# The last feed-forward in pairs of tiles, issued between the steps of the multi-head attention

## The chip, the cores and the metric

One core of one Trainium2 chip runs the whole program. The metric is device microseconds (us) of one execution; lower is better. Engines are called as in the profile: PE is TensorE (PEld its weight loads), DVE VectorE, ACT ScalarE, POOL GpSimd, SP the engine that issues the loads and stores here.

## The reference

Eight tiles of 128 tokens with 256 features go through two layers. Cut to what is computed:

```python
x = x + tanh(g_xattn[0]) * L0_xattn(layernorm(x), ctx, mask)       # stage A, one head
x = x + tanh(g_ffn[0])   * L0_ffn(layernorm(x), w1, w2, w3)        # stage B, quantised
x = x + tanh(g_xattn[1]) * L1_xattn(layernorm(x), ctx, ...)        # stage C, 16 heads, own layernorm of the result
x = x + tanh(g_ffn[1])   * L1_ffn(layernorm(x), w_gate, w_up, w_down)   # stage D
# L1_ffn: down(silu(x @ w_gate.T) * (x @ w_up.T)); hidden width 1024
```

All of it is fp32. Stage D splits each operand into a high and a low part in a one-pass matmul type and adds three products (high by high, low by high, high by low).

## The kernel before, in words

Each engine has one written order of instructions; semaphores join them. An engine that waits holds up everything behind it in its own order. The stages A, B and C go tile by tile: `step_c(t, p)` is called for t = 0 to 9 on every engine, and in one call each engine does its part for several tiles at different points of their way.

What happens to tile u in stage C, with the names used below:

- `xt_c(u)`: PE transposes the normed tile, ACT copies it out (`copy_ht`). `q(u)`: the query projection; ACT adds the bias and masks heads (`q_out`).
- `scores(u)`: PE writes banks 0 to 3; ACT takes four exponentials of 512 columns (`exp_c`); DVE clips the probabilities (L742, "the clip").
- `heads`: PE sums the probabilities of each head (head sums, bank 7) and multiplies them by the values (head values, bank 6). DVE takes the reciprocal of the sums (L728) and multiplies (OT, L735).
- PE multiplies by the output weights (`delta`, L1222, bank 5), DVE scales it (DL, L749), takes its mean and variance, POOL takes the power -0.5 (L373), DVE makes D2 (L762) and adds it to X (L769).
- Then the norm for stage D: statistics of X on DVE, power on POOL (L289), `norm_d` on DVE (XD, L714), two transposes on PE (XD), `hi_d` on ACT (L959), `lo_d` on DVE (L720). HTH and HTL, the two parts of the transposed tile, are what stage D reads.

Stage D goes over two groups of four tiles (TG = 512 tokens) and eight blocks of 128 hidden columns in each, 16 blocks n in all. `gate_up_d(n)`: 12 matmuls of 512 columns, gate into one bank and up into another, two pairs of banks in turn. ACT takes silu of gate (`silu_d`, L993), DVE multiplies by up (`gu_d`, L699), ACT rounds the high part (`hi_gu`, L997), DVE subtracts for the low part (`lo_gu`, L707), PE adds the block's share to the result (`down_d`, L1278, 12 matmuls of 256 columns). PE issues `down_d(n)`, then `gate_up_d(n + 2)`. At the end of each group DVE adds the result to X (`update_d`, L784), and SP stores pairs of tiles. Only two `gate_up_d` are issued inside the last steps of stage C:

```python
if t == NT:
    pe.wait_ge(c_ex, 4 * NT)
    gate_up_d(0)
...
for n in range(NG * FC):
    if n == 2:
        step_c(NT + 1, 1)
    down_d(n)
    if n + 2 < NG * FC:
        gate_up_d(n + 2)
```

ACT holds one table of functions: exp and silu lie in different ones, and `warm(func)` is a one-element call that brings the other table in ahead of use. Stage C runs under exp, stage D under silu, with one switch between them.

## Time and profile before

| | |
|---|---|
| median of 3 runs | 264.27 us (264.17 to 264.46) |
| the profiled execution | 264.11 us |
| its span (first to last instruction) | 262.3 us |
| granted PE clock, mean | 0.946 of full speed |
| PE busy | 212.0 us, 81% of the span |
| DVE, ACT, POOL busy | 181.0, 132.8, 83.9 us |

Stage C starts at about 127 us, the first block of stage D at 184.6 us, and the last matmul at 258.45 us. All times below are of the span of this one execution. A matmul's duration in the trace contains its way through the array, so the pace of a row of matmuls is read from one start to the next, not from the sum of durations.

### The profile page before, as it was taken

The page shows a single profiled execution, that of the slowest core. Times are in us where ns is not written, and L with a number is a line of the kernel's source. Part 1 is how long each engine was busy: PE and PEld are TensorE (multiplying, and loading weights), DVE is VectorE, ACT ScalarE, POOL GpSimd, SP SyncE. Part 2 cuts the span into 40 slices and gives each one's busy share as a digit, 9 for nine tenths or more (in the row PEclk, how much of TensorE's full clock was granted, in tenths as well). Part 3 has the DMA queues.
Part 4 walks back from the last instruction along what each step waited for, and adds up shares of the span by engine and source line. Part 5 has one row for each costly group of instructions (what it writes and reads, how often), then busy time and mean ns, then how long its engine had stood idle before and what let it go on. Part 6 is the DMA issues. An engine that isn't in the chain of part 4 may idle for free.

```text
span 262.3 us, 4538 instructions
## 1 busy us (share of the span) xinstructions
PE 212.0 (81%) x1658; PEld 174.5 (67%) x1658; DVE 181.0 (69%) x457; ACT 132.8 (51%) x296; POOL 83.9 (32%) x108
## 2 busy tenths in 40 slices
PE   0285557979889889897798688775999999999992
PEld 0264325858778778786576466654877888888882
DVE  2769879598988988786428999998984333262333
ACT  1138874478667667679755455553322323222220
POOL 2301111175856856868505333442100000000000
PEclk9999955699999999999959999997999999999999
DMA  5999003900000000000000000000000000020002
GB/s 169 369 390 301 5 0 139 343 1 0 2 0 0 2 1 0 2 2 0 0 2 2 0 2 4 0 4 0 2 2 0 0 0 2 0 80 2 0 0 80
DMA packets 9238, 12.55 MB, mean 48 GB/s; under 512 B 1025, under 2 KB 7937, under 8 KB 9217
## 3 DMA queue, kind: packets, MB, share of 16 engines
q1 hardware_dynamic: 8784, 12.07, 13.3%
q10 hardware_dynamic: 432, 0.20, 0.4%
q8 instruction: 13, 0.21, 0.3%
q14 instruction: 9, 0.07, 0.1%
HBM read 11.22 MB, written 1.05 MB: 47 GB/s over the span
## 4 chain that ended last, share of the span: by engine, by line
PE 50%; DVE 27%; ACT 7%; DMA 6%; issue 4%; POOL 3%; SPq 1%; DVEq 0%; ACTq 0%; POOLq 0%
PE PB L1259 16%; PE PB L1278 7%; DMA WRAW<-w_dram 6%; PE PB L1073 6%; PE PB L1172 4%; PE PB L1085 3%; DVE XV L524 3%; PE PB L1108 2%; PE PB L1112 2%; DVE HBQ L742 2%; PE PB L1019 2%; DVE RD L728 2%; DVE HBQ L572 2%; ACT SIL L906 2%; DVE HSD L578 2%
## 5 line engine op out<-in xcount | busy, mean ns | idle before, releaser
L1259 PE MATMUL PB<-SGN,WHI 128*128 128x512 f32 x128 | 40.5, 397 | 0.0
L1073 PE MATMUL PB<-SGN,XQH 128*128 128x512 f32 x64 | 27.7, 433 | 1.3 <-DVE XQL L553 1.3
L699 DVE TENSOR_TENSOR WRAW<-WRAW,PB 128x512 f32<-128x512 f32 x16 | 11.0, 686 | 24.0 <-ACT WRAW L993 23.9
L1278 PE MATMUL PB<-WHI,SGN 128*128 128x256 f32 x128 | 25.6, 283 | 2.2 <-DVE SGN L707 1.8
L1073 PE MATMUL PB<-SGN,XQL 128*128 128x512 f32 x64 | 27.1, 424 | 0.0
L289 POOL TENSOR_TENSOR RSTD<-MVS,MHALF 128x1 f32<-128x1 f32 x24 | 13.4, 560 | 40.9 <-DVE MVS L401 40.9
L1259 PEld LDWEIGHTS PB<-SGN,WHI 128*128 128x128 f32 x128 | 22.9, 188 | 4.5 <-issue 0.2
L1259 PE MATMUL PB<-SGN,WLO 128*128 128x512 f32 x64 | 25.2, 394 | 0.0
L993 ACT ACTIVATE WRAW<-PB 128x512 f32<-128x512 f32 x16 | 9.6, 600 | 28.0 <-PE PB L1259 28.0
L1278 PEld LDWEIGHTS PB<-WHI,SGN 128*128 128x128 f32 x128 | 20.7, 188 | 3.6 <-DVE SGN L707 2.4
L316 POOL TENSOR_TENSOR HBQ<-HBQ,HR 128x512 f32<-128x512 f32 x16 | 17.6, 1098 | 17.2 <-DVE HR L590 17.2
L906 ACT ACTIVATE SIL<-PB,WSC 128x512 f32<-128x512 f32 x16 | 11.0, 688 | 20.5 <-PE PB L1073 16.9
L322 POOL TENSOR_TENSOR HBQ<-HBQ,HSD 128x512 f32<-128x512 f32 x16 | 17.0, 1063 | 13.6 <-ACT HBQ L915 13.6
L572 DVE SCALAR_TENSOR_TENSOR HBQ<-PB,WSC,SIL 128x512 f32<-128x512 f32 x16 | 12.0, 747 | 10.9 <-ACT SIL L906 10.8
L707 DVE TENSOR_TENSOR SGN<-WRAW,SGN 128x512 fp32r<-128x512 f32 x16 | 11.1, 693 | 11.0 <-ACT SGN L997 11.0
L997 ACT CAST SGN<-WRAW 128x512 fp32r<-128x512 f32 x16 | 9.9, 620 | 17.1 <-DVE WRAW L699 17.1
L1019 PE MATMUL PB<-ident,XH 128*128 128x128 f32 x32 | 7.4, 327 | 13.6 <-DVE XH L417 13.6
L728 DVE RECIPROCAL RD<-PB 128x256 f32<-128x256 f32 x8 | 14.0, 1752 | 5.8 <-PE PB L1172 5.8
L1085 PE MATMUL PB<-SGN,HQH 128*128 128x256 f32 x64 | 18.0, 313 | 0.0
L1278 PE MATMUL PB<-WLO,SGN 128*128 128x256 f32 x64 | 17.9, 280 | 0.0
L1172 PE MATMUL PB<-HBQ,ONE 128*32 128x128 f32 x256 | 10.2, 308 | 9.0 <-DVE D L762 9.0
L966 ACT ACTIVATE HBQ<-PB 128x512 f32<-128x512 f32 x32 | 17.5, 616 | 0.0
(122 smaller groups left out, 545.7 us busy)
## 6 DMA issues: line engine op xcount, KB each, us to landing
WRAW<-w_dram SPq DMA_DIRECT2D x2, 2048.0 KB, 12.1
X<-x_dram SPq DMA_DIRECT2D x2, 512.0 KB, 5.8
CTXT<-ctxt_dram SPq DMA_DIRECT2D x1, 1024.0 KB, 9.6
CTX<-ctx_dram SPq DMA_DIRECT2D x1, 1024.0 KB, 12.0
WRAW<-w_dram SPq DMA_DIRECT2D x1, 1024.0 KB, 14.9
WQK<-wqkvo_dram SPq DMA_DIRECT2D x1, 1024.0 KB, 7.8
WRAW<-wd_dram SPq DMA_DIRECT2D x1, 1024.0 KB, 10.1
out_dram<-X SPq DMA_DIRECT2D x4, 256.0 KB, 2.2
```

The lines of the kernel that those rows point to most:

```text
L289: nc.gpsimd.tensor_tensor(RSTD[:, bass.ds(t, 1)], MVS[:, bass.ds(t, 1), 1], MHALF[:], ALU.pow).then_inc(rstd_ready, 1)
L316: nc.gpsimd.tensor_tensor(h, h, spread(HR, p, half), ALU.mult).then_inc(b_v, 1)
L322: nc.gpsimd.tensor_tensor(halves(HQ, p, half), halves(HB, p, half), spread(HSD, p, half), ALU.mult).then_inc(b_hq, 1)
L572: nc.vector.scalar_tensor_tensor(out=h_part(p, half), in0=PB[2 * half + 1][:], scalar=WSC[:, 1:2], in1=SIL[:, half, :], op0=ALU.mult, op1= ...
L728: nc.vector.reciprocal(RD[:], PB[7][:, 0:D]).then_inc(c_rd, 1)
L906: nc.scalar.activation(SIL[:, half, :], PB[2 * half][:], ACT.Silu, scale=WSC[:, 0:1]).then_inc(b_sil, 1)
L966: nc.scalar.activation(PR[:, p, b * 512:(b + 1) * 512], PB[b][:], ACT.Exp, scale=1.0 / math.sqrt(HD)).then_inc(c_ex, 1)
L1073: mm = nc.tensor.matmul(PB[2 * half + m][:], part[:, p, c, :], sgn(m, c, a, b), start=(c == 0 and k == 0), stop=(c == DC - 1 and k == 1))
L1085: mm = nc.tensor.matmul(PB[7][:, 0:D], part[:, j, :], sgn3(j), start=(j == 0 and i == 0), stop=(j == FC - 1 and i == 1))
L1172: mm = nc.tensor.matmul(PB[bank][HB32 * j:HB32 * (j + 1), c * P:(c + 1) * P], parts(h), PR[:, p, head_at(h):head_at(h) + P], start=(e == 0 ...
L1259: mm = nc.tensor.matmul(PB[2 * b + m][:], wcol(w_part, m, c, j), act_part[:, c, g * TG:(g + 1) * TG], start=(c == 0 and i == 0), stop=(c = ...
L1278: mm = nc.tensor.matmul(down_bank(g, k), act_part[:, b, ts], wdown(w_part, j), start=(j == 0 and i == 0 and k % 2 == 0), stop=(j == FC - 1 ...
```

## The change

Stage D works on pairs of tiles (TG = 256 tokens, four groups of eight blocks, 32 blocks n). Gate and up of a block share one bank, 256 columns each. Blocks up to n = 16 use bank 6 alone; later ones take turns between banks 6 and 0. `down_d` has 6 matmuls of 256 columns. Four buffers instead of two hold the products.

The blocks are issued inside `step_c`: in step t, n = 4t - 14, each engine does its part of blocks n to n + 3 among its work for stage C, and of `down_d` blocks n - 3 to n; t runs to 11. The first blocks, 0 and 1, fall into step 3; blocks 2 to 13 into steps 4 to 6; the attention's own work ends with step 9.

To make room in PSUM, head sums and head values share bank 5 with `delta`, the transposes of XD move to bank 4 (shared with `xt_c` and `q`), and the result of `down_d` has bank 7. The reciprocal waits for the head values (c_pv) instead of for the sums alone.

The exponentials of tile t + 1 are taken in step t instead of step t + 1. The mean and variance of DL, D2, the update of X, and the statistics of X of a tile move one step later on DVE, to the start of the step, and `norm_d` and `lo_d` follow in the same step. ACT switches tables twice in each of the steps 3 to 6 (exp for the four exponentials, silu after them), and once more in step 3.

PE's order in a step t from 4 to 6 is: `down_d(n-3)`, `q(t+1)`, `down_d(n-2)`, `gate_up_d(n)`, head sums (t-1), XD transposes (t-2), `gate_up_d(n+1)`, head values (t-1), `down_d(n-1)`, `gate_up_d(n+2)`, `scores(t+1)`, `xt_c(t+2)`, `gate_up_d(n+3)`, `delta(t-1)`, `down_d(n)`.

The core of the diff (DVE's order first, then ACT's, then two functions of PE, whose order is given above; of the removed lines only the first stand here):

```diff
-TG = 512
-NG = NT * P // TG
-TPG = TG // P
+TPG = 2
+TG = TPG * P
+NG = NT // TPG
+NB = 4
+SPT = NG * FC // NT
+LEAD = 14
+LAST = (LEAD + NG * FC) // SPT + 1
...
+        def gu_bank(n):
+            return PB[6] if n <= SPT * NT // 2 or n % 2 == 0 else PB[0]
+        def ffn(n):
+            return 0 <= n < NG * FC
...
-                sp.wait_ge(x_done, 2 * i + 3 * NT + 2)
+                sp.wait_ge(d_x, i + 1)
...
+            def update_d(g):
+                dve.wait_ge(d_dn, FC * (g + 1))
+                xs = X[:, TPG * g:TPG * (g + 1), :].rearrange("p t d -> p (t d)")
+                nc.vector.scalar_tensor_tensor(
+                    out=xs, in0=PB[7][:], scalar=TANHG[:, 3:4], in1=xs, op0=ALU.mult,
+                    op1=ALU.add).then_inc(d_x, 1)
...
             def step_c(t, p):
+                n = SPT * t - LEAD
+                if live(t - 2):
+                    dve.wait_ge(c_de, t - 1)
+                    nc.vector.bn_stats(ST2[:], DL[:]).then_inc(c_st, 1)
+                    dve.wait_ge(c_st, t - 1)
+                    nc.vector.bn_aggr(MV2[:], ST2[:]).then_inc(c_mv, 1)
+                    dve.wait_ge(c_mv, t - 1)
+                    nc.vector.tensor_scalar(VE2[:], MV2[:, 1:2], LN_EPS, None, ALU.add
+                                            ).then_inc(c_ve, 1)
+                if n > FC and (n - 2) % FC == 0:
+                    update_d((n - 2) // FC - 1)
+                if live(t - 2):
+                    nc.vector.scalar_tensor_tensor(
+                        out=D2[:], in0=DL[:], scalar=MV2[:, 0:1], in1=GAM[:],
+                        op0=ALU.subtract, op1=ALU.mult).then_inc(c_d2, 1)
+                if ffn(n - 1):
+                    gu_d(n - 1)
+                if live(t - 2):
+                    dve.wait_ge(c_d2, t - 1)
+                    dve.wait_ge(c_r2, t - 1)
+                    dve.wait_ge(c_xb, t - 1)
+                    nc.vector.scalar_tensor_tensor(
+                        out=X[:, t - 2, :], in0=D2[:], scalar=RSTD2[:], in1=X[:, t - 2, :],
+                        op0=ALU.mult, op1=ALU.add).then_inc(x_done, 1)
+                    stats(t - 2, p, t - 2 + 2 * NT)
+                if ffn(n - 1):
+                    lo_gu(n - 1)
+                if ffn(n):
+                    gu_d(n)
+                if live(t - 2):
+                    norm_d(t - 2)
+                if ffn(n):
+                    lo_gu(n)
+                if live(t - 2):
+                    lo_d(t - 2)
                 if live(t + 2):
                     norm(t + 2, p, 2)
+                if ffn(n + 1):
+                    gu_d(n + 1)
+                if live(t - 1):
...
+                if ffn(n + 1):
+                    lo_gu(n + 1)
+                if ffn(n + 2):
+                    gu_d(n + 2)
                 if live(t):
...
+                if ffn(n + 2):
+                    lo_gu(n + 2)
                 if live(t - 1):
                     dve.wait_ge(c_dl, t)
...
+            def silu_d(n):
+                act.wait_ge(d_gu, n + 1)
+                nc.scalar.activation(SG[:, n % NB, :], gu_bank(n)[:, 0:TG], ACT.Silu
+                                     ).then_inc(d_sil, 1)
+            def hi_gu(n):
+                act.wait_ge(d_g, n + 1)
+                need(act, d_dn, n - NB + 1)
+                nc.scalar.copy(GUH[:, n % NB, :], GU[:, n % NB, :]).then_inc(d_gh, 1)
...
             def step_c(t, p):
+                n = SPT * t - LEAD
+                switch = ffn(n + 3) and live(t + 1)
                 if live(t + 1):
                     q_out(t + 1)
+                if ffn(n):
+                    silu_d(n)
+                    hi_gu(n)
+                if live(t - 2):
+                    hi_d(t - 2)
+                if ffn(n + 1):
+                    silu_d(n + 1)
+                    hi_gu(n + 1)
+                if switch and not ffn(n + 2 - SPT):
+                    warm(ACT.Silu)
+                if ffn(n + 2):
+                    silu_d(n + 2)
+                if switch:
+                    warm(ACT.Exp)
+                if live(t + 1):
+                    exp_c(t + 1, 1 - p, 0)
+                if ffn(n + 2):
+                    hi_gu(n + 2)
+                if live(t + 1):
+                    exp_c(t + 1, 1 - p, 1)
                 if live(t + 2):
                     copy_ht(t + 2, p, 4, xt_done, c_q, c_ht, 2 * NT)
+                if live(t + 1):
+                    exp_c(t + 1, 1 - p, 2)
+                    exp_c(t + 1, 1 - p, 3)
+                if switch:
+                    warm(ACT.Silu)
+                if ffn(n + 3):
+                    silu_d(n + 3)
+                    hi_gu(n + 3)
             warm(ACT.Exp)
             copy_ht(1, 1, 4, xt_done, c_q, c_ht, 2 * NT)
...
+            for b in range(4):
+                exp_c(0, 0, b)
+            for t in range(LAST):
+                step_c(t, t % 2)
...
+            def xd_t(u):
+                pe.wait_ge(d_ln, u + 1)
+                need(pe, d_hl, u)
+                pe.wait_ge(c_qm, 4 * min(u + 4, NT))
+                transpose_x(XD[:], 4, d_t)
+            def gate_up_d(n):
+                g, j = n // FC, n % FC
+                if j == 0:
+                    pe.wait_ge(d_hl, TPG * (g + 1))
+                if n == SPT * NT // 2 + 1:
+                    pe.wait_ge(c_ex, 4 * NT)
+                elif n > SPT * NT // 2:
+                    pe.wait_ge(d_g, n - 1)
+                else:
+                    need(pe, d_g, n)
+                for m in range(2):
+                    terms = ((HTH, WHI), (HTL, WHI), (HTH, WLO))
...
```

## Rows read from the trace of the kernel before

**Rows 1.** The chain that ended last: shares of the span by engine

```profile
PE 50%; DVE 27%; ACT 7%; DMA 6%; issue 4%; POOL 3%; SPq 1%; DVEq 0%; ACTq 0%; POOLq 0%
```

**Rows 2.** Busy time in stretches of stages C and D

```profile
core 0: us, PE busy (x) PEld busy (x) DVE busy (x) ACT busy (x) POOL busy (x), PEclk, DMA share, GB/s
...
131.70:139.50 7.80, 7.34 (x91) 5.77 (x90) 2.96 (x5) 3.84 (x9) 1.02 (x2) 0.56 0.01 2
...
153.90:161.10 7.20, 5.60 (x96) 4.54 (x96) 6.96 (x16) 4.10 (x10) 2.77 (x6) 1.00 0.00 1
...
212.00:231.00 19.00, 19.00 (x113) 16.66 (x112) 6.21 (x9) 6.09 (x10) 0.00 (x0) 1.00 0.00 1
```

**Rows 3.** Timeline of one steady step of stage C (start, duration, instruction)

```profile
151.90 1.75 DVE L728 RECIPROCAL RD<-PB 128x256 f32<-128x256 f32 x1
...
156.89 1.52 ACT L898 ACTIVATE QM<-PB,BQM,PAR 128x128 f32<-128x128 f32 x4
...
157.83 0.49 DVE L769 SCALAR_TENSOR_TENSOR X<-D,RSTD,X 128x256 f32<-128x256 f32 x1
...
157.94 1.08 PE L1172 MATMUL PB<-HBQ,ONE 128*32 128x128 f32 x32 [1.43 <-DVE D L762]
...
159.10 1.75 DVE L728 RECIPROCAL RD<-PB 128x256 f32<-128x256 f32 x1
159.26 0.55 POOL L289 TENSOR_TENSOR RSTD<-MVS,MHALF 128x1 f32<-128x1 f32 x1 [1.56 <-DVE MVS L401]
```

**Rows 4.** Timeline of the start of stage C

```profile
125.97 1.09 ACT L966 ACTIVATE HBQ<-PB 128x512 f32<-128x512 f32 x2
...
126.93 1.05 PE L1160 MATMUL PB<-HT,WQK 128*128 128x128 f32 x8
...
129.47 1.10 ACT L966 ACTIVATE HBQ<-PB 128x512 f32<-128x512 f32 x2
...
132.72 2.08 PE L1160 MATMUL PB<-HT,WQK 128*128 128x128 f32 x8 [0.46 <-ACT HT L821]
...
136.73 1.76 DVE L728 RECIPROCAL RD<-PB 128x256 f32<-128x256 f32 x1 [4.84 <-PE PB L1172]
...
140.87 0.48 DVE L749 SCALAR_TENSOR_TENSOR DL<-PB,RES,BO 128x256 f32<-128x256 f32 x1 [0.62 <-PE PB L1222]
```

**Rows 5.** Timeline of one steady block of stage D

```profile
217.60 0.64 PE L1259 MATMUL PB<-SGN,WHI 128*128 128x512 f32 x2
...
220.41 0.28 PE L1278 MATMUL PB<-WHI,SGN 128*128 128x256 f32 x1
...
220.60 0.60 ACT L993 ACTIVATE WRAW<-PB 128x512 f32<-128x512 f32 x1 [2.24 <-PE PB L1259]
...
221.81 0.64 PE L1259 MATMUL PB<-SGN,WHI 128*128 128x512 f32 x2
```

**Rows 6.** Timeline around the two switches of ACT's table

```profile
124.09 1.28 ACT L813 ACT_TABLE_LOAD   x1
...
125.62 0.37 ACT L821 COPY HT<-PB 128x256 f32<-128x256 f32 x1
...
185.33 1.28 ACT L813 ACT_TABLE_LOAD   x1
...
187.80 0.60 ACT L993 ACTIVATE WRAW<-PB 128x512 f32<-128x512 f32 x1 [0.97 <-PE PB L1259]
```

**Rows 7.** Groups of instructions by line and shape (count, busy, mean ns of one)

```profile
L735 DVE TENSOR_TENSOR OT<-PB,RD 128x256 f32<-128x256 f32 x8 | 3.4, 419 | 0.1
...
L959 ACT CAST SGN<-PB 128x256 fp32r<-128x256 f32 x8 | 3.0, 372 | 16.6 <-PE PB L1019 16.6
```

**Rows 8.** Timeline of the end

```profile
258.07 1.66 DVE L784 SCALAR_TENSOR_TENSOR X<-PB,TANHG,X 128x256 f32<-128x256 f32 x4 [1.06 <-PE PB L1278]
...
258.45 0.28 PE L1278 MATMUL PB<-WHI,SGN 128*128 128x256 f32 x1
```

More of the change, by code:

```diff
@@ L999, in _ @@
[L999 to L1009 removed]
+            for b in range(4):
+                exp_c(0, 0, b)
+            for t in range(LAST):
+                step_c(t, t % 2)
         @block.tensor
@@ L1192, in scores, with head_sums, head_values, delta @@
                             mm.then_inc(c_s, 1)
+            def head_sums(u, p):
+                pe.wait_ge(c_p, u + 1)
+                need(pe, c_de, u)
+                heads(0, lambda h: ONE2[:, h % 2, :], p)
+            def head_values(u, p):
+                pe.wait_ge(c_v, 2 * u + 2)
+                heads(D, lambda h: V1[:, p, h, :], p).then_inc(c_pv, 1)
+            def delta(u):
+                pe.wait_ge(c_o, u + 1)
+                for c in range(DC):
+                    mm = nc.tensor.matmul(PB[5][:, 0:D], OT[:, c * P:(c + 1) * P],
+                                          WQK[:, 3, c, :], start=(c == 0), stop=(c == DC - 1))
+                mm.then_inc(c_dl, 1)
@@ new lines, in xd_t @@
+            def xd_t(u):
[15 more added lines that the diff above has]
+                    terms = ((HTH, WHI), (HTL, WHI), (HTH, WLO))
+                    for c in range(DC):
+                        for i, (act_part, w_part) in enumerate(terms):
+                            mm = nc.tensor.matmul(
+                                gu_bank(n)[:, m * TG:(m + 1) * TG], wcol(w_part, m, c, j),
+                                act_part[:, c, g * TG:(g + 1) * TG],
+                                start=(c == 0 and i == 0), stop=(c == DC - 1 and i == 2))
+                mm.then_inc(d_gu, 1)
@@ new lines, in down_d @@
+            def down_d(n):
+                g, j = n // FC, n % FC
+                pe.wait_ge(d_gl, n + 1)
+                if j == 0:
+                    need(pe, d_x, g)
+                for k in range(TPG):
+                    ts = slice(k * P, (k + 1) * P)
+                    terms = ((GUH, WHI), (GUH, WLO), (GUL, WHI))
+                    for i, (act_part, w_part) in enumerate(terms):
+                        mm = nc.tensor.matmul(
+                            PB[7][:, k * D:(k + 1) * D], act_part[:, n % NB, ts],
+                            wdown(w_part, j), start=(j == 0 and i == 0 and k == 0),
+                            stop=(j == FC - 1 and i == 2), skip_group_check=True)
+                mm.then_inc(d_dn, 1)
@@ L1215, in step_c @@
                     xt_c(t + 2, p)
-                if t == NT:
-                    gate_up_d(1)
+                if t >= NT:
+                    down_d(n)
+                if ffn(n + 3):
+                    gate_up_d(n + 3)
                 if live(t - 1):
-                    pe.wait_ge(c_o, t)
-                    need(pe, c_de, t - 1)
-                    for c in range(DC):
-                        mm = nc.tensor.matmul(PB[5][:, 0:D], OT[:, c * P:(c + 1) * P],
-                                              WQK[:, 3, c, :], start=(c == 0),
-                                              stop=(c == DC - 1))
-                    mm.then_inc(c_dl, 1)
-                if live(t - 2):
-                    pe.wait_ge(d_ln, t - 1)
-                    if not live(t - 1):
-                        pe.wait_ge(d_hl, t - 2)
-                    transpose_x(XD[:], 7, d_t)
+                    delta(t - 1)
+                if t < NT and ffn(n):
+                    down_d(n)
+                if t >= NT:
+                    down_d(n + 1)
             pe.wait_ge(b_xl, NT)
```

194 lines of the change are left out of this document (45 added, 149 removed).

## Prediction

> **What bounds the kernel now.** I read the chain that ended last first: half of it is PE and a quarter DVE [rows 1], so no single engine explains the span and the stages have to be taken apart. The windows do that [rows 2]. In a steady step of stage C DVE is busy 6.96 of 7.20 us and PE 5.60. In stage D, once it runs, PE is busy all the time. So stage C waits for DVE, stage D for PE, and running them side by side could in principle fill PE's 1.6 us of idle time per step of C.
>
> The steady timeline gives the pace: one reciprocal to the next is 7.20 us [rows 3]. A block of stage D takes 221.81 - 217.60 = 4.21 us for 12 matmuls of 512 columns (220.41 - 217.60 = 2.81, so 234 ns each) and 12 of 256 columns (1.40, 117 ns each) [rows 5]. A column costs the same in both widths.
>
> PE's side of the ledger: from q(1) at 126.93 [rows 4] to the end of the last matmul, 258.45 + 0.28 [rows 8], are 131.8 us. The work in it is 16 x 4.21 = 67.4 for stage D and 8 x 5.60 less some 2.8 for what was issued earlier (q(0), scores(0), two transposes) = 42.0. That is 109.4 us. The other 22.4 us are waits and a half clock. The change has to bring that number down. It cannot touch the 109.4.
>
> **Part by part: PE's work.** The change doubles the number of gate and up matmuls at half the width: 32 x 12 x 0.117 = 44.9 us, as 16 x 2.81 before, and `down_d` stays at 32 x 6 x 0.117 = 22.5. Cost nothing, on the row. The doubled weight loads (192 more) lie under the matmuls, as they do in the 256-column `down_d`, whose pace is exactly half; without that cover 192 x 0.188 (a weight load's own time there) would be 36 us, which the 117 ns excludes.
>
> **ACT and DVE per block.** For 256 columns I take 0.40 us for an ACT operation (0.372 for the 256-column cast) and 0.42 for a DVE one (0.419) [rows 7]. Both engines together do more small instructions than before, but neither is full: DVE 7.2 + 8 x 0.42 = 10.6 us a step, ACT 4.1 + 8 x 0.40 and two switches. What counts is the order in which they answer PE.
>
> **The table switches.** A load takes 1.28 us, and 125.62 - 124.09 = 1.53 us pass from its start to the next operation [rows 6]. I take 1.53. The other switch has 2.47 us to the next operation, but there 0.97 of it is a wait for PE, so 2.47 is the upper bound. Nine switches replace one. ACT's idle time covers their sum (about 14 us); their place does not hide them all, as the next part shows. The Trainium skill ("ScalarE: Activation LUTs", What ACT_TABLE_LOAD costs, and its rule to batch by table set) speaks against the edit: it gives 1283 ns for the load, which the trace shows, and some 1380 ns of draining besides, 2.66 us for each switch. No row shows that drain. By the page's price each switch would take 1.13 us more, two in each of four steps, and the sum would come to about 273.
>
> **An interleaved step (t = 4 to 6), walked in order.** PE has 13.95 us of work: four gate_up of 1.40, four `down_d` of 0.70, 5.55 for attention (5.60 in the row [rows 2]; split by starts in the steady step: q 1.0, head sums 0.87 of the 1.08 shown [rows 3], values 1.0, scores 1.05, `xt_c` 0.35, delta 0.95, XD 0.35). Set 0 at the start of `gate_up_d(n+3)` of the step before. PE goes on with delta, down, down, q, down until 5.45 and then needs bank 6 free, that is `gu_d` of that last block. Its silu stands on ACT behind a chain that starts with the silu of the block before (gate_up from -2.8; its result 1.6 later, since silu followed 0.19 after the last matmul was issued, 220.60 against 220.41 [rows 5]; silu to -0.8): switch to exp (0.76), exponential, `hi_gu`, exponential, `copy_ht`, two exponentials at 0.545 each [rows 4] (3.65), switch to silu (5.18), silu (5.57), `gu_d` (6.02). With 0.1 for a start after a wait, PE goes on at 6.1: **0.65 us lost**. The second place: after gate_up(n) and head sums PE is free at 8.37 for the XD transposes, which need `norm_d`. On DVE that stands behind `gu_d(n)`, which needs silu(n), which on ACT stands behind `q_out` (1.4, from 6.45) [rows 3]: silu ends 8.24, `gu_d` 8.69, `norm_d` 9.06, transposes 9.15: **0.78 us lost**. After that PE runs through (values, down, gate_up, scores, transposes) to the next gate_up at 15.4. So a step costs 15.4 us. The same work before cost 7.20 + 4 x 2.11 = 15.6. The interleaving as such gives only 0.2 us a step; a PE without waits would give 1.65.
>
> **The start (steps 0 and 1).** All four exponentials of tile 0 now run at once, 125.97 to 128.15, where the second pair waited to 129.47 [rows 4]. q(2) then starts at about 131.4 and not 132.72. In that stretch the granted clock was 0.56, the lower level of 1.2 GHz for most of it, after a thinly used PE, and it came back after PE had been full [rows 2]. I let it fall again: q(2) 2.0, head sums 1.6, values 1.0 at the restored clock, ending at 136.0. The reciprocal now needs the values, so it starts at 136.1 and not at 136.73, and DL of tile 0 at 139.5 and not 140.87. A gain of 1.4; half a microsecond if the values are slow too.
>
> **Steps 2 and 3, without cover.** Here the moved chain stands bare on DVE. The update of X waits for POOL's power (0.25). `norm_d` comes right after the statistics, and from the update's start to the end of the second power are 159.81 - 157.83 = 1.98 us, where DVE has 1.27 of work [rows 3]: 0.7 lost. `lo_d` comes right after `norm_d` and waits for PE's transposes and ACT's cast: 1.5 from start to start where 0.4 is work: 1.1 lost. Before, the clip and the reciprocal (1.75) lay over these waits. With 0.15 for delta that makes 9.4 us from DL of tile 0 to that of tile 1, at 148.9, against 7.2 a step before. In step 3 the first gate_up waits for the same `lo_d` and starts at 6.05 after DL, scores follow, and the second gate_up starts at 8.85: 157.75.
>
> **The sum.** Second gate_up of step 3 at 157.75; of step 4, 5 and 6 at 173.2, 188.6 and 203.65 (step 6 has one transpose pair less). From there 49.75 us of PE work remain (19 gate_up, 22 `down_d`, three tiles' rest). To it come 1.35 (no q to cover the switch to silu in step 7) and 0.6, 1.4 and 1.95 at the XD transposes of tiles 5, 6 and 7, where `norm_d` again ends DVE's chain of some 4 us after DL; and 0.5 before the last `down_d`. That ends PE at 259.1, and 22.5 us of waits stand where 22.4 stood. The last update is one instruction of 512 columns, at most the 0.83 that two tiles took [rows 8]: 259.95, against 258.07 + 1.66 = 259.73. So the profiled execution goes from 264.11 to 264.3; the median stood 0.16 above it: **264.5 us**.
>
> **Rivals.** (a) *The waits find cover and PE binds.* If `norm_d` and the silu are ready a little earlier than my walk has them, the interleaved steps fall towards 13.95: three times 1.43 gone is 4.3 us, **260.2**. For it: each wait is under 0.8 us, two or three instructions long. Against: both hang on ACT's written order. It decides where a step takes under 15.2.
> (b) *The clock falls in steps 2 and 3*, and this is the case on the other side. PE works in bursts there, with two gaps of over 1.5 us, as it did in bursts ahead of the fall at the start [rows 2, 4]; in the steady step, with a longest gap of 1.43 [rows 3], the clock stayed at 1.00 [rows 2]. At half rate the two gate_up, scores and delta in the path (1.4 + 1.4 + 1.1 + 1.0) take up to 4.9 more; with part of the stretch covered I take 3: **267.5**. It decides from the point at which a gate_up of step 3 takes over 2 us.
> (c) *A switch costs the upper bound*, 2.47: 0.94 more, twice in the chain that PE waits for, four times: 7.5 us, **272**. The rule on draining in the Trainium skill's page on ScalarE's tables would do this. The 1.53 us at the switch without a wait speak against it.
>
> **Chances.** Forecast case, gains and waits cancelling to within 1.5 us: 0.45 (faster 0.14, same 0.16, slower 0.15). (a) 0.25, (b) 0.24, (c) 0.06. Faster by over 0.2% (half a microsecond, about what a measurement of this kernel can tell): 0.14 + 0.25 = 0.39. Same 0.16. Slower 0.15 + 0.24 + 0.06 = 0.45. The range takes in (a) and (b) with little to spare: 260.0 to 268.0, leaving out (c) and the ends of (a) and (b), about 0.18. My forecast's own range is 263.0 to 266.0.
>
> **What the profile after would show.** Right: the second gate_up of one step to that of the next 15.2 to 15.6 us; PE waiting for DVE's `gu_d` before the first gate_up of a step and for `norm_d` before XD's transposes, 0.6 to 0.8 each; eight or more loads of 1.28 us; the DVE step from DL 0 to DL 1 over 9 us; gate_up at 117 ns a matmul. Wrong: PE over 95% busy from step 4 on (then (a)); a clock under 0.9 between 140 and 160 us (then (b)); silu over 2 us after a load's start (then (c)); or 256-column gate_up slower than 117 ns, which would add 4.5 us for each 10% and is the one term I hold certain.

## The result, and the profile after

| | before | changed |
|---|---|---|
| median | 264.37 us (264.17 to 264.83, 4 runs) | 268.41 us (267.57 to 269.21, 4 runs) |
| profiled execution, its span | 264.11, 262.3 us | 267.57, 265.8 us |
| mean granted clock | 0.946 | 0.949 |

The ratio is 1.015, with an interval of 1.0113 to 1.0188: the changed kernel is 1.5% slower, and 0.4 us past the upper end of the range. Its four executions, from the fastest to the slowest, have mean clocks of 0.949, 0.949, 0.939 and 0.932; the profiled one is the fastest, so the 0.8 us from it to the median are not profiled. The forecast for the profiled execution was 264.3, so 3.3 us have to be found in it. Ratios, and the medians below, leave out executions more than 1.5% above the fastest of their kernel: three of the nine of e1, its profiled one among them, and two of before's.

The start of stage C, from the timeline (it answers to [rows 4]; the load to [rows 6]):

```profile
125.35 1.28 ACT L820 ACT_TABLE_LOAD   x1
...
127.23 2.06 ACT L973 ACTIVATE HBQ<-PB 128x512 f32<-128x512 f32 x4
...
128.20 1.06 PE L1179 MATMUL PB<-HT,WQK 128*128 128x128 f32 x8
...
133.04 1.16 PE L1179 MATMUL PB<-HT,WQK 128*128 128x128 f32 x8 [1.05 <-ACT HT L828]
...
136.16 1.76 DVE L783 RECIPROCAL RD<-PB 128x256 f32<-128x256 f32 x1 [4.40 <-PE PB L1191]
...
139.60 0.48 DVE L801 SCALAR_TENSOR_TENSOR DL<-PB,RES,BO 128x256 f32<-128x256 f32 x1
```

All four exponentials run at once, as drawn. Two things were not drawn. The load itself stands at 125.35 and not at 124.09, though nothing ahead of it was changed. And q(2) takes 1.16 us, not 2.08: here the clock did not fall. The two cancel, and DL of tile 0 comes at 139.60 (forecast 139.5).

Then the steps. PE's timeline from step 3 on, first the waits of steps 3 and 4, then the last gate_up, `gate_up_d(n + 3)`, of steps 3 to 6. It is the second one of step 3 and the fourth of the others; the prediction says "second" of all, but its walk goes from one `gate_up_d(n + 3)` to the next.

```profile
154.27 0.44 PE L1037 MATMUL PB<-ident,XD 128*128 128x128 f32 x2 [2.12 <-DVE XD L730]
155.63 0.50 PE L1251 MATMUL PB<-SGN,WHI 128*128 128x256 f32 x2 [0.92 <-DVE SGN L736]
...
164.44 0.50 PE L1251 MATMUL PB<-SGN,WHI 128*128 128x256 f32 x2 [1.51 <-DVE WRAW L708]
...
167.40 0.44 PE L1037 MATMUL PB<-ident,XD 128*128 128x128 f32 x2 [0.25 <-DVE XD L730]
```

```profile
158.53 0.48 PE L1251 MATMUL PB<-SGN,WHI 128*128 128x256 f32 x2
...
173.82 0.48 PE L1251 MATMUL PB<-SGN,WHI 128*128 128x256 f32 x2
...
189.06 0.48 PE L1251 MATMUL PB<-SGN,WHI 128*128 128x256 f32 x2
...
204.10 0.51 PE L1251 MATMUL PB<-SGN,WHI 128*128 128x256 f32 x2
```

Forecast were 157.75, 173.2, 188.6 and 203.65. Up to 204 us the profile is 0.45 us behind the walk. The rest of the 3.3 us lies behind that. PE's timeline there, and the windows around it (columns as in [rows 2]):

```profile
239.10 0.53 PE L1037 MATMUL PB<-ident,XD 128*128 128x128 f32 x2 [2.12 <-DVE XD L730]
239.29 0.77 PE L1251 MATMUL PB<-SGN,WHI 128*128 128x256 f32 x2
...
242.00 0.41 PE L1267 MATMUL PB<-WHI,SGN 128*128 128x256 f32 x1
...
243.04 0.40 PE L1251 MATMUL PB<-SGN,WHI 128*128 128x256 f32 x2
...
245.19 0.40 PE L1251 MATMUL PB<-SGN,WHI 128*128 128x256 f32 x2
...
246.62 0.28 PE L1267 MATMUL PB<-WHI,SGN 128*128 128x256 f32 x1
```

```profile
236.00:239.00 3.00, 0.98 (x9) 0.78 (x7) 2.54 (x9) 1.09 (x3) 1.00 (x2) 1.00 0.01 3
239.00:242.00 3.00, 2.90 (x15) 2.90 (x16) 0.80 (x3) 0.37 (x1) 0.00 (x0) 0.55 0.00 0
242.00:243.00 1.00, 1.00 (x7) 1.00 (x7) 0.35 (x1) 0.38 (x1) 0.00 (x0) 0.64 0.05 16
243.00:251.00 8.00, 8.00 (x69) 8.00 (x68) 3.60 (x9) 2.70 (x7) 0.00 (x0) 1.00 0.10 33
```

PE waits 2.12 us for `norm_d` of tile 7, and on the far side the granted clock is 0.55, close to the lower level of 1.2 GHz. The gate_up that starts at 239.29 takes 242.00 - 239.29 = 2.71 us and the `down_d` after it 1.04; in the block of 245.19, at full clock, these are 1.43 and 0.71. That is 1.6 us gone beside the wait itself. A block at full clock takes 2.14 us here, where half a block of before took 2.11 [rows 5].

The end, from the timeline (it answers to [rows 8]):

```profile
261.45 0.39 PE L1267 MATMUL PB<-WHI,SGN 128*128 128x256 f32 x1 [0.41 <-DVE SGN L715]
...
262.48 0.75 DVE L722 SCALAR_TENSOR_TENSOR X<-PB,TANHG,X 128x512 f32<-128x512 f32 x1 [1.08 <-PE PB L1267]
```

### The profile page after: what moved, and what is told of

Its sections match the earlier page's. It is cut to its first block and busy times, and to the rows that moved or that the text cites. A ratio compares the mean times of both kernels' runs of the same rounds, so it can differ in the third digit from the quotient of the medians.

```text
span 265.8 us, 5038 instructions
## 1 busy us (share of the span) xinstructions
PE 216.3 (81%) x1850; PEld 185.1 (70%) x1850; DVE 185.8 (70%) x485; ACT 150.2 (57%) x344; POOL 84.8 (32%) x108
## 5 line engine op out<-in xcount | busy, mean ns | idle before, releaser
L1251 PE MATMUL PB<-SGN,WHI 128*128 128x256 f32 x256 | 49.7, 291 | 3.8 <-DVE WRAW L708 2.9
L1251 PEld LDWEIGHTS PB<-SGN,WHI 128*128 128x128 f32 x256 | 40.2, 193 | 5.2 <-DVE WRAW L708 4.0
L1251 PE MATMUL PB<-SGN,WLO 128*128 128x256 f32 x128 | 36.6, 286 | 0.0
L1267 PE MATMUL PB<-WHI,SGN 128*128 128x256 f32 x128 | 29.0, 297 | 0.5 <-DVE SGN L715 0.4
L978 ACT ACTIVATE WRAW<-PB 128x256 f32<-128x256 f32 x32 | 12.3, 385 | 27.5 <-PE PB L1251 27.4
L708 DVE TENSOR_TENSOR WRAW<-WRAW,PB 128x256 f32<-128x256 f32 x32 | 13.4, 419 | 18.5 <-ACT WRAW L978 18.5
L984 ACT CAST SGN<-WRAW 128x256 fp32r<-128x256 f32 x32 | 12.9, 405 | 21.4 <-DVE WRAW L708 21.4
L1251 PEld LDWEIGHTS PB<-SGN,WLO 128*128 128x128 f32 x128 | 24.6, 192 | 0.0
L382 POOL TENSOR_TENSOR RSTD<-VE,MHALF 128x1 f32<-128x1 f32 x8 | 5.4, 678 | 53.1 <-DVE VE L749 53.1
L715 DVE TENSOR_TENSOR SGN<-WRAW,SGN 128x256 fp32r<-128x256 f32 x32 | 13.5, 422 | 8.5 <-ACT SGN L984 7.9
## 6 DMA issues: line engine op xcount, KB each, us to landing
WRAW<-w_dram SPq DMA_DIRECT2D x2, 2048.0 KB, 12.2
CTX<-ctx_dram SPq DMA_DIRECT2D x1, 1024.0 KB, 12.2
```

Source lines behind the costliest of these rows:

```text
L708: nc.vector.tensor_tensor(GU[:, b, :], SG[:, b, :], gu_bank(n)[:, TG:2 * TG], ALU.mult).then_inc(d_g, 1)
L715: nc.vector.tensor_tensor(GUL[:, b, :], GU[:, b, :], GUH[:, b, :].bitcast(F32), ALU.subtract).then_inc(d_gl, 1)
L978: nc.scalar.activation(SG[:, n % NB, :], gu_bank(n)[:, 0:TG], ACT.Silu).then_inc(d_sil, 1)
L984: nc.scalar.copy(GUH[:, n % NB, :], GU[:, n % NB, :]).then_inc(d_gh, 1)
L1251: mm = nc.tensor.matmul(gu_bank(n)[:, m * TG:(m + 1) * TG], wcol(w_part, m, c, j), act_part[:, c, g * TG:(g + 1) * TG], start=(c == 0 and ...
L1267: mm = nc.tensor.matmul(PB[7][:, k * D:(k + 1) * D], act_part[:, n % NB, ts], wdown(w_part, j), start=(j == 0 and i == 0 and k == 0), stop ...
```

## The experiments

Each kernel runs with before on the same chip; before had medians of 263.96 beside e1 to e4, 264.12 beside e5 to e8, 264.19 beside e9 and e10, and 264.18 beside e11. "Over before" is the difference of the two medians, and kernels are compared by it. The first columns are of these runs; the others are of the profiled execution, in us counted from its exp table load: DL of tiles 0, 1 and 7, and the end of the last update.

| kernel | median | over before | ratio to before | load at | DL 0 | DL 1 | DL 7 | end |
|---|---|---|---|---|---|---|---|---|
| before | 264.37 | | | 124.09 | 16.78 | 24.44 | 69.39 | 135.64 |
| before again (e0) | 264.59, one run | | | 124.52 | 16.78 | 24.45 | 69.47 | 135.72 |
| changed | 268.41 | 4.0 | 1.0113 to 1.0188 | 125.35 | 14.25 | 24.07 | 108.82 | 137.88 |
| e1 no switch | 265.08 | 1.1 | 1.0017 to 1.0087 | 125.50 | 15.83 | 26.60 | 108.39 | 137.41 |
| e2 XD later | 264.22 | 0.3 | 0.9973 to 1.0026 | 125.22 | 15.86 | 26.30 | 108.93 | 135.49 |
| e3 keep clock | 266.31 | 2.4 | 1.0064 to 1.0116 | 124.82 | 14.23 | 25.00 | 109.66 | 137.19 |
| e4 pairs only | 268.24 | 4.3 | 1.0144 to 1.0237 | 125.58 | 15.71 | 23.35 | 66.09 | 137.38 |
| e5 early exp | 262.24 | -1.9 | 0.9900 to 0.9958 | 124.53 | 15.11 | 22.77 | 67.01 | 133.27 |
| e7 step later | 272.22 | 8.1 | 1.0269 to 1.0373 | 124.59 | 14.24 | 25.00 | 105.13 | 141.62 |
| e8 fill early | 263.84 | -0.3 | 0.9956 to 1.0011 | 124.30 | 16.84 | 26.34 | 108.98 | 135.53 |
| e9 fill start | 261.47 | -2.7 | 0.9831 to 0.9922 | 124.84 | 13.51 | 21.16 | 66.26 | 132.49 |
| e10 tanh | 267.36 | 3.2 | 1.0074 to 1.0154 | 125.18 | 15.84 | 26.28 | 110.43 | 138.51 |
| e11 all mended | 262.76 | -1.4 | 0.9920 to 0.9976 | 126.06 | 14.23 | 23.74 | 106.37 | 132.95 |

**The 1.26 us ahead of the load.** Two kernels ask whose they are: before once more, and before with 192 narrow matmuls at its end, so that it has as many PE instructions as the changed one.

> The kernel before, unchanged, for one more profile of it. Theory 1 (the 1.3 us by which the changed kernel's profile is later at the first exp table load are the place of the clock's half stretch in stages A and B, which moves from run to run): the load lies somewhere between 124.1 and 125.6 us, and the half stretch between 20 and 55 us with it. Rival (they belong to the changed program): it stands at 124.1 us again, within 0.1.

> The kernel before with 192 more matmuls of 32 columns at its end, into a bank that nothing reads: as many TensorE instructions as the changed kernel has, and some 6 to 10 us more work at the end, so its time says nothing. What is read is the first exp table load, which stands at 124.09 us in before and at 124.82 to 125.58 us in the changed kernel and its four variants. Theory 1 (a longer program moves the first loads, and the clock's half stretch with them): it stands at 125.2 us or later. Rival (it is the clock's half stretch of that one run, or of those kernels for another reason): it stays at 124.1 us, or lies wherever the half stretch between 20 and 55 us of that run puts it.

The load stood at 124.52 in the first and at 125.03 in the second; in e5 and e9, the same as before up to there, at 124.53 and 124.84. Windows of before and then of before again:

```profile
20.00:30.00 10.00, 5.30 (x30) 3.67 (x28) 9.06 (x42) 8.74 (x33) 1.67 (x3) 1.00 0.64 189
30.00:40.00 10.00, 5.64 (x17) 2.87 (x17) 7.54 (x31) 7.60 (x26) 1.71 (x3) 0.64 0.00 0
```

```profile
20.00:30.00 10.00, 5.48 (x31) 3.85 (x29) 9.09 (x42) 8.74 (x33) 1.66 (x3) 0.99 0.64 189
30.00:40.00 10.00, 6.51 (x16) 3.72 (x17) 7.17 (x31) 7.64 (x26) 1.70 (x3) 0.50 0.00 0
```

The stretch at half clock in stages A and B does not start in the same place in each execution, and moves all that follows. From the load on, the two executions of before agree to 0.1 us. The load is at 124.09 to 125.03 in the five profiles that have before's program up to there and its groups of four, at 124.30 to 126.06 in the nine others. In all fourteen it is later the longer the stretch lasts: the mean clock from 20 to 60 us is 0.79 in before (load at 124.09), 0.74 in three (124.30 to 124.53), 0.70 in seven (124.59 to 125.35), 0.66 in two (125.50 and 125.58) and 0.62 in e11 (126.06). So e0's theory 1 held; of e6 the theory (125.2 or later) missed and the rival held, by which the load lies where the stretch puts it. The second group's mean is higher by 0.5 us (125.13, without e4, against 124.60); whether the changed program lengthens the stretch stays open. The 192 matmuls of e6 took 38.2 us where 6 to 10 were expected; the last section comes back to them. All comparisons of profiles below count from the load.

**The clock in the tail (e3).** Idle matmuls ahead of the XD transposes of steps 8 and 9:

```diff
+                if live(t - 2) and t >= NT:
+                    for _ in range((6, 16)[t - NT]):
+                        nc.tensor.matmul(PB[1][:, 0:TG], wcol(WHI, 0, 0, 0), HTH[:, 0, 0:TG],
+                                         start=True, stop=True)
                 if live(t - 2):
                     xd_t(t - 2)
```

> The changed kernel with 6 and 16 idle matmuls of 256 columns into a free bank ahead of the transposes of XD in steps 8 and 9, so that PE is busy while it waits. Theory (the wait itself is unchanged, but the clock falls after it and costs 1.5 us): gate_up 23 takes 1.43 instead of 2.71 us and the time falls by 1 to 2 us. Rival (the clock falls anyway or the fall is not what separates the runs): within 0.5 us of the changed kernel, or slower.

266.31, 2.4 us over before where the changed kernel is 4.0 over: 1.7 us less, as its theory had it. The same place in its windows, PE filled and the clock whole:

```profile
235.00:238.00 3.00, 3.00 (x28) 3.00 (x27) 2.66 (x9) 0.69 (x2) 0.72 (x1) 1.00 0.01 3
238.00:241.00 3.00, 2.79 (x25) 2.59 (x23) 1.93 (x6) 0.78 (x2) 0.68 (x1) 1.00 0.02 5
241.00:244.00 3.00, 3.00 (x28) 3.00 (x27) 0.97 (x3) 1.17 (x3) 0.00 (x0) 1.00 0.00 0
```

From DL of tile 7 to the end are 27.53 us and not 29.06: 1.53 us, the 1.6 read above. So the price of the fall is shown twice over. That the fill is what kept the clock does not follow from this one profile, because the clock can stay whole without it. e1 has the same wait of 2.12 us there and the same fall; e7 waits 2.23 us, unfilled, and has none:

```profile
235.06 0.44 PE L1037 MATMUL PB<-ident,XD 128*128 128x128 f32 x2 [2.23 <-DVE XD L730]
```

```profile
232.00:235.00 3.00, 0.82 (x6) 0.62 (x6) 2.71 (x10) 1.09 (x3) 0.68 (x1) 1.00 0.26 87
235.00:238.00 3.00, 2.94 (x25) 2.95 (x26) 1.18 (x4) 0.92 (x3) 0.00 (x0) 1.00 0.00 0
```

The count of filled and open waits in the last section speaks for the fill.

**The order around XD (e2).** PE takes gate_up(n+1) ahead of the transposes; ACT takes silu(n+1) ahead of `hi_d`, DVE the norm and `gu_d(n+1)` ahead of `lo_d`. PE's part:

```diff
-                if live(t - 2):
-                    xd_t(t - 2)
                 if ffn(n + 1):
                     gate_up_d(n + 1)
+                if live(t - 2):
+                    xd_t(t - 2)
```

> The changed kernel with the transposes of XD one place later on PE (after gate_up n+1), and hi_d and lo_d one place later on ACT and DVE. Theory (PE stands still for norm_d although work is ready): the waits of 0.25 three times, 0.24, 0.94 and 2.12 us before these transposes shrink to under 1 us in all, and with them goes the fall of the clock after the longest; the time falls by 2.5 to 4 us, to about 265. Rival (the work behind, gate_up n+1 and then gate_up 24, waits for gu_d and lo_d instead): less than 1 us is gained.

264.22: 3.8 us less over before than the changed kernel, level with before, as its theory had it. PE's waits from 160 to 260 us, in all, times, longest:

```profile
PE PB L1252 <- DVE WRAW L708: 2.9, 3, 1.5
PE PB L1038 <- DVE XD L730: 0.7, 1, 0.7
PE PB L1268 <- DVE SGN L715: 0.4, 1, 0.4
```

The XD waits are down to one of 0.7, the clock stays whole in the tail (26.56 us from DL 7 to the end), and this with a worse start, where the clock did fall (DL 0 at 15.86).

**The switches (e1, e10).** e1 takes exp of gate in place of silu and has no loads in the steps; it leaves silu out, and only its time counts.

> The changed kernel without its nine extra switches of ACT's table: the silu of the feed-forward is replaced by an exponential, so that all of it runs under one table (the output is therefore not that of the reference). Theory (switches in ACT's order hold up PE at the start of a step): PE's waits before the first gate_up of steps 4 and 7 (1.51 and 1.07 us in the changed kernel's trace) and the 0.31 of step 5 go, and the time falls by 2.5 to 3.5 us to about 265. Rival (the waits only move on to the transposes of XD, because norm_d is late anyway): less than 1 us is gained. A second rival, that each switch costs more than the 1.5 us seen: more than 5 us is gained.

265.08, 2.9 us less over before than the changed kernel, as its theory had it. PE's waits for the product and for XD from 160 us to the end, in the changed kernel and then in e1: the first go, the second stay, so the rival is out.

```profile
PE PB L1251 <- DVE WRAW L708: 2.9, 3, 1.5
PE PB L1037 <- DVE XD L730: 4.0, 6, 2.1
```

```profile
PE PB L1245 <- DVE WRAW L708: 0.6, 1, 0.6
PE PB L1031 <- DVE XD L730: 4.2, 6, 2.1
```

Its profiled execution has a mean clock of 0.923, with falls ahead of 154 us and again at 239; the steps between these, at full clock, from DL 2 to DL 5 (38.29, 52.38, 67.05, 81.83 us after the load), take 14.1, 14.7 and 14.8 us, against 15.3, 15.25 and 15.05 (35.76, 51.05, 66.30, 81.35). So the switches cost about 2 us over these three steps. e10 takes them away in a kernel that computes silu: the Trainium skill ("ScalarE: Activation LUTs", Table sets: the hidden batching unit) puts exp and tanh in one set, and this case's profile agrees (its first stage takes both under one load). DVE pays with one more instruction a block, on top of e2:

```diff
-                nc.vector.tensor_tensor(GU[:, b, :], SG[:, b, :], gu_bank(n)[:, TG:2 * TG],
-                                        ALU.mult).then_inc(d_g, 1)
+                nc.vector.scalar_tensor_tensor(
+                    out=SG[:, b, :], in0=SG[:, b, :], scalar=1.0, in1=gu_bank(n)[:, 0:TG],
+                    op0=ALU.add, op1=ALU.mult).then_inc(d_s1, 1)
+                dve.wait_ge(d_s1, n + 1)
+                nc.vector.scalar_tensor_tensor(
+                    out=GU[:, b, :], in0=SG[:, b, :], scalar=0.5, in1=gu_bank(n)[:, TG:2 * TG],
+                    op0=ALU.mult, op1=ALU.mult).then_inc(d_g, 1)
```

> The variant with the XD transposes behind the second gate and up block (264.2 us), with silu(g) worked out as g / 2 * (1 + tanh(g / 2)): exp and tanh lie in one table (the profile shows a tanh and the exponentials of the first stage with no load between), so the switches in steps 3 to 6 fall away, and VectorE takes one more instruction of 256 columns for each block. Theory 1 (the switches cost some 2 us, as the variant without them suggested, and VectorE has room): a step of the interleaved ones falls from 15.0 to about 14.4 us and the time to 262.0 to 263.2. Rival (VectorE's added 0.45 to 0.5 us a block stands in the same chain from gate and up to the freed bank, and takes the gain back): 264 to 265.5 us, with longer waits of TensorE for VectorE's product ahead of gate and up.

267.36, 3 us more than e2 and past its rival too. Its waits from 160 to 260 us:

```profile
PE PB L1252 <- DVE WRAW L713: 3.3, 7, 1.0
PE PB L1038 <- DVE XD L736: 1.6, 2, 1.4
PE PB L1252 <- DVE SGN L742: 0.5, 1, 0.5
```

The wait for the product comes seven times instead of three, 0.4 us more in all, and those at XD are 0.9 us longer. ACT's switches were cheaper than 0.42 us more on DVE in each block.

**The parts alone (e4, e5, e7).** e4 is before with pairs of tiles (TG = 256, gate and up still in two banks), nothing interleaved. e5 is before with the exponentials a step earlier. e7 is the changed kernel with LEAD = 18, four blocks fewer between the steps and four more behind them.

```diff
-                if live(t):
-                    exp_c(t, p, 0)
-                    exp_c(t, p, 1)
                 if live(t + 1):
                     q_out(t + 1)
-                if live(t):
-                    exp_c(t, p, 2)
-                    exp_c(t, p, 3)
+                    exp_c(t + 1, 1 - p, 0)
+                    exp_c(t + 1, 1 - p, 1)
                 if live(t + 2):
                     copy_ht(t + 2, p, 4, xt_done, c_q, c_ht, 2 * NT)
+                if live(t + 1):
+                    exp_c(t + 1, 1 - p, 2)
+                    exp_c(t + 1, 1 - p, 3)
```

> The kernel before with pairs of tiles alone (TG = 256, four groups, gate and up in banks of their own, the blocks behind the attention as before, nothing interleaved). Theory (a 256-column gate_up matmul takes 119.5 ns here and not 117): 384 times 2.5 ns is 1.0 us slower than before, about 265.3. Rival (the narrower matmul costs nothing, as my prediction had it): within 0.4 us of before. A second rival: four groups also need shorter waits at the end, and it is faster by 0.5 to 1.

> The kernel before with one part of the change alone: the exponentials of tile t+1 are issued in step t (those of tile 0 ahead of step 0). The feed-forward, its groups of four tiles and its two banks stay where they were. Theory 1 (the start pays as forecast): the first residual (DL of tile 0) comes 1.2 to 1.4 us earlier than the 140.87 us of the profiled run of before, counted from the first exp table load, and the kernel ends about 1.2 us sooner: 262.5 to 263.2 beside the 264.0 of before on this chip. Rival (TensorE sets the pace anyway, or the clock takes it back): the steady steps keep their 9.4 to 9.8 us and the end comes within 0.4 us of before. Whichever holds, the place of the exp table load tells about the shift ahead of the attention: this kernel has the same instructions as before up to there, so it should stand at 124.1 us if the shift of 1.3 us in the changed kernels belongs to them, and anywhere from 124 to 125.6 us if it moves from run to run.

> The changed kernel with the whole feed-forward one step later (18 in place of 14 blocks behind), so that four blocks fewer lie between the attention's steps. Theory 1 (a block between the steps costs as much TensorE time as one behind them, 2.14 us, and the steps only hide 0.2 to 0.4 us of waits each): 268 to 269 us, within 0.5 us of the changed kernel's 268.4. Rival (the interleaving does hide waits, about 2 us a step): 270 to 271 us.

e4 is slower by as much as the whole change, 4.3 us, and its theory and both rivals missed. Its blocks take 2.14 us instead of 2.11, and at the change of stages, where two blocks are in flight, a block of half the work covers half as much of the chain over ACT and DVE; PE's waits there:

```profile
192.30 0.36 PE L1276 MATMUL PB<-WHI,SGN 128*128 128x256 f32 x1 [0.68 <-DVE DL L749]
...
196.42 0.38 PE L1276 MATMUL PB<-WHI,SGN 128*128 128x256 f32 x1 [1.73 <-DVE SGN L707]
```

Before has 0.45 and 0.40 in these two places. The profiled execution is the fastest of its four and ends 1.75 us later than before's, counted from the load; the load is 1.49 us later besides. Where the rest of the 4.3 lies was not profiled. e5 is faster by 0.7%, 1.9 us, more than its theory's 1.2. DL 0 comes 1.7 us earlier after the load (1.2 to 1.4 expected); how much of that is the order and how much a shorter stretch at half clock there (the windows below) is not separated. Its profile gains another 0.7 between DL 5 and DL 6, where the clock fell in before (0.52 from 179.5 to 183 us) and not in e5. In e7 the rival held, by a little more than its figures: 4.0 us slower over before than the changed kernel. The four blocks are 8.56 us of PE work; taken from between the steps they shorten the time to DL 7 by 3.7 us and lengthen the tail by 7.4. So blocks between the steps do hide waits, about a microsecond each. The two profiles have falls of the clock in different places, e7 from 145 to 162 us and the changed one at 239; without them 3.7 would be some 4.6 (DL 0 to DL 1 takes 0.95 longer in e7) and 7.4 some 9.0, an estimate, with much the same difference.

**Filling the other falls (e8, e9, e11).** e8 is e2 with idle matmuls in the waits of steps 1 to 3. e9 is e5 with 8 of them ahead of scores(1) and 8 ahead of q(2). e11 is e8 with those two as well.

```diff
             def step_c(t, p):
+                if t == 1:
+                    for _ in range(8):
+                        nc.tensor.matmul(PB[5][:, 0:D], wcol(WHI, 0, 0, 0), WHI[:, 1, 0:D],
+                                         start=True, stop=True)
                 if live(t + 1):
                     q(t + 1, 1 - p)
+                if t == 0:
+                    pe.wait_ge(b_hl, 2 * NT)
...
```

> The variant in which the transposes of XD come behind the second gate and up block of a step, with idle 256-column matmuls put where TensorE waits in the first steps: 7 ahead of the output projection of steps 1 and 2, 16 and 8 ahead of the XD transposes of steps 2 and 3. Theory 1 (the half clock at 133 to 138 us and 147 to 154 us of that variant costs what TensorE does there at half speed, and comes from its waits): the clock stays whole from 126 us to the end, and the time falls by 1.5 to 2.5 us from 264.2 to 261.7 to 262.7 us, under both kernels. Rival (VectorE's chain of the first steps sets the time there, at either clock): within 0.5 us of 264.2 us. A third: the idle matmuls themselves come late and hold up the work behind them: 264.5 to 265.5 us.

> The kernel before with the exponentials one step earlier (262.24 us on this chip) and, besides, 8 idle 256-column matmuls ahead of scores(1) and 8 ahead of q(2), where TensorE waits about 1.0 us each. Theory 1 (the half clock at 131 to 137 us comes from these waits, and costs q(2) and the head sums there 1.7 us, which the first DL passes on): the granted clock stays whole from 126 to 145 us, the first DL comes 14.0 us after the exp table load and not 15.1, and the time falls by about 1 us, to 261.0 to 261.6. Rival (the clock falls there whatever TensorE does in these two gaps): within 0.3 us of 262.24, the first DL at 15 to 16 us after the load.

> The interleaved kernel with everything mended that the runs have shown so far: the XD transposes behind the second gate and up block, idle matmuls in the waits of steps 1 to 3 (263.8 us with these two), and the 8 and 8 idle matmuls ahead of scores(1) and q(2) that kept the clock whole at the start of the plain kernel with early exponentials (261.47 us there). Theory 1 (the early exponentials and the whole clock give the gain, the interleaving of pairs gives nothing beside them): the first DL comes 13.5 us after the exp table load where it came 14.3 to 16.8, the end some 132.5 to 133.5 us after the load, and the time is 261.0 to 262.3, level with 261.47. Rival (the interleaving earns its own 1 to 2 us once the clock is whole): 259.3 to 260.5 us. A third (VectorE's chain in steps 2 and 3 eats the earlier start): 263 to 264 us.

e8 gained nothing that can be told from no change. The clock stood whole from 138.2 us on, but had fallen before that (0.53 from 131 to 138.2), and the step from DL 0 to DL 1 is 9.5 us at full clock as well: there DVE's chain is the limit, its rival. e9 has the lowest median of this study, 261.47, and its theory held; its interval and that of e5 just overlap. Windows of e5, then of e9:

```profile
126.00:132.00 6.00, 4.16 (x42) 2.77 (x34) 2.79 (x6) 5.13 (x13) 3.42 (x5) 1.00 0.00 0
132.00:138.00 6.00, 5.71 (x88) 4.76 (x88) 1.94 (x3) 2.72 (x8) 1.02 (x3) 0.72 0.01 3
```

```profile
126.00:132.00 6.00, 5.95 (x64) 4.76 (x57) 3.04 (x8) 5.12 (x13) 3.33 (x6) 1.00 0.00 0
132.00:138.00 6.00, 5.73 (x98) 4.48 (x96) 3.23 (x4) 4.31 (x12) 1.87 (x4) 1.00 0.01 3
```

PE filled in the first row, the clock whole in the second, DL 0 1.6 us earlier. The end gains 0.8: between DL 5 and DL 6 half of it is given back (7.85 us in place of 7.00). There PE waits 2.3 us ahead of the head sums of tile 7 in both, and behind it the clock fell in e9 and not in e5. Windows of e5, then of e9:

```profile
177.00:180.00 3.00, 1.80 (x64) 1.72 (x64) 2.83 (x9) 0.00 (x0) 1.03 (x2) 1.00 0.00 0
```

```profile
177.00:180.00 3.00, 3.00 (x60) 3.00 (x64) 2.15 (x5) 0.00 (x0) 1.25 (x2) 0.50 0.02 5
```

e11 beats both kernels too, at 262.76, 0.5 us over the upper end of its theory 1 and under the third's; its DL 0 comes at 14.23 and not at 13.5. From the load its end is 132.95, beside 132.49 of e9, although its clock stood whole from 126 to 258 us and that of e9 did not. Beside the early exponentials and the idle matmuls the interleaving of pairs, as it stands here, has no gain to show.

## Why the prediction was wrong

- **Ahead of the change**: the sum took the load's place from one execution of before. It moved by 1.26 us in the changed kernel's, by 0.4 in a second one of before, and by 0.9 in one with the same program up to there (e6). No term stood for that, and it is over a third of the 3.3 us. A term of the other sign hides it up to DL 0: the clock that stayed at the start (below) gives 1.1 us back.
- **"Cost nothing, on the row"**, for gate_up in 256 columns, "the one term I hold certain": 1.435 us a block, 119.5 ns a matmul and not 117. Over 32 blocks 32 x 1.435 - 16 x 2.81 = 1.0 us, 5 ns for each of the 192 added matmuls. The forecast took the 117 ns of `down_d`'s 256 columns for gate_up's; `down_d` keeps them in both kernels, so the width alone does not set the pace, and why gate_up is slower stays open. The Trainium skill ("TensorE: Matmul & The Clock Gate", Wait — 56ns, not 53.3ns?) states a fixed cost of some 2.5 ns for each matmul beside its columns; by it the term would be 0.5 us, an estimate of the right sign and half the size. The trace does not bear out one cost for every matmul: `down_d` at 256 columns shows none beside the 234 ns of 512.
- **ACT and DVE per block**: 0.40 and 0.42 were taken; the page after shows 385 ns (silu), 405 (`hi_gu`), 419 and 422 (`gu_d`, `lo_gu`). Right.
- **The switches**: 1.53 from a load's start to the next operation. Right, now where ACT goes on with silu, and the exponentials ahead of the load end at 162.00:

```profile
162.01 1.28 ACT L820 ACT_TABLE_LOAD   x1
163.31 0.20 ACT L820 ACTIVATE WARM<-TANHG 128x1 f32<-128x1 f32 x1
163.54 0.38 ACT L978 ACTIVATE WRAW<-PB 128x256 f32<-128x256 f32 x1
```

  Rival (c) is out, and with it the draining in the price of the Trainium skill's page ("ScalarE: Activation LUTs", What ACT_TABLE_LOAD costs).
- **The interleaved step**, 15.4 us: 15.29, 15.24, 15.04. Right, but by two errors that cancel. Its two losses were put at 0.65 and 0.78; the first is 1.51, 0.31 and nothing in steps 4 to 6, the second 0.25, 0.24 and 0.24. So in steps 5 and 6 PE loses 0.55 and 0.24 us where 1.43 stood, and its work takes 14.7 where 13.95 stood: there is no term for the 0.1 to 0.2 us that a block takes longer when PE comes from another kind of work.
- **The start**: a gain of 1.4 was forecast with a fallen clock. In the profiled execution the clock stayed (2.5 us gained from the load to DL 0); in e1, e2 and e10, which have the same program there, it fell, and DL 0 came 15.8 us after the load, 0.95 gained. e3 and e7 have 14.23, with the clock whole, as in the changed kernel's profile. The order was read rightly; which clock meets it changes by the execution.
- **The bare step**: 9.4 from DL 0 to DL 1, measured 9.82.
- **The sum's last leg is the step that failed**: "49.75 us of PE work remain", plus 5.8 of waits. From 204.10 to the end of the last matmul at 262.44 are 58.3 us, and its terms add to 55.55 (the forecast's own end, 259.1, leaves 55.45). That is 2.8 too many: 1.6 for the clock behind the wait at 239.10; 0.7 for the pace (18 gate_up by 0.035, 22 `down_d` by 0.005); 1.0 less for waits (4.8 in all); and 1.5 left over. The sum has no term for these, and the trace shows them as 0.1 to 0.2 us wherever PE starts after a wait or with another kind of work, as the gate_up of 213.02 that takes 1.61. A wait of 1.95 us stood in the forecast, at this place. That the clock could fall behind it was told only of steps 2 and 3.
- **Rival (b)** had the mechanism, and its 267.5 is nearest to the result, but partly by luck. In the profiled execution the waits of 2.1 us in steps 2 and 3 passed at full clock, and the fall came in the tail. That execution is the exception: in the other five interleaved profiles with these waits open (e1, e2, e3, e7, e10) the clock did fall there, in e2 to 0.62 from 146 to 150 us and 0.53 from 150 to 154. It cost less than the 3 us taken: DL 0 to DL 1 is 10.4 to 10.8 us there and 9.82 at full clock, and DL 1 to DL 2 stays at 11.7 in e1, e2 and e3. In the same place, then, the clock falls in one execution and not in another.
- **Rival (a)**, PE without waits, did not come: 17.3 us of waits of PE stand between 126 us and the end. e2, with 12.2, ends level with before.

Why the change does not pay, then: it bundles a part that gains (the early exponentials, 1.9 us alone), a part that hides waits (a block between the steps costs about half of one behind them, e7), and parts that lose. The losers are the bare steps 2 and 3 of 9.5 us and more, where a step of before takes 7.2 [rows 3] (read from the traces, no run takes them out); the smaller matmuls, 1.0; the switches, 2 to 3 (e1); and the waits at XD with the clock that falls behind them, 3.8 in the medians (e2). These numbers overlap and are not a sum: e4's loss in particular has a part (the change of stages) that the changed kernel doesn't have.

## What to carry to other kernels

Split a change into its parts and time each: here the smallest edit, an order of four instructions on ACT, held the whole gain, and 16 idle matmuls seem to add to it (0.8 us, at the edge of what the intervals tell apart). A forecast that has PE wait for 2 us must price the clock on the far side at every such place, not only at the one where the waits are most, and must say how far the start of the stage itself moves from one execution to the next. When two engines share a chain, look at which of them has the room before work is moved from one to the other: ACT's two table loads a step cost less than one more instruction a block on DVE.

## What the runs showed of the hardware that was not expected

- The granted clock fell, and stayed at its lower level of 1.2 GHz, while PE was listed as busy without a gap. The added matmuls of e6 have 32 columns, each behind its own 128-column weight load, and run from 259.5 us to the end: 111 ns apart up to 262.4 us, 213 ns behind that. PE had waited 1.4 us for `lo_gu` up to 257.9; whether that wait or the narrow matmuls brought the fall is not shown, but no gap stands behind it. The windows:

```profile
240.00:250.00 10.00, 10.00 (x56) 8.60 (x55) 3.45 (x5) 2.75 (x5) 0.00 (x0) 1.00 0.01 2
...
258.00:262.40 4.40, 4.40 (x39) 4.40 (x40) 1.66 (x4) 0.00 (x0) 0.00 (x0) 1.00 0.36 119
...
266.00:275.00 9.00, 9.00 (x44) 9.00 (x44) 0.00 (x0) 0.00 (x0) 0.00 (x0) 0.50 0.00 0
```

- The stretch at half clock in stages A and B moves between two executions of one program (the load at 124.09 and 124.52 us in before), and the load by up to 0.9 us between kernels that have before's program up to there (e6), and by 1.8 between those that have the changed one's (124.30 in e8, 126.06 in e11).
- There are four places where PE waits 1 to 2.3 us and the clock fell in most executions, but not where the wait was filled with idle 256-column matmuls. (In before's steady steps, with waits of 1.43 us, it stayed whole.) Counted over the fourteen profiles: with the waits open it fell at the start of stage C in 9 of 12, in steps 2 and 3 in 5 of 6, ahead of the head sums of tile 7 in before's order in 4 of 6, and at XD of tile 7 in the tail in 2 of 3. Filled, it fell in none of 5 (the start in e9 and e11, steps 2 and 3 in e8 and e11, the tail in e3). The counts are small.
